# Sheaf edge loop: 80 of 125 columns summed on TensorE instead of 70, column sums laid between the equality sums, 16-bit source rows

## The reference

```python
h = jnp.maximum(_layernorm(x), 0.0)                     # (12500, 16)
xs, xd = h[src], h[dst]                                 # per edge, 16 values each
def reflection(a, b):
    return jax.nn.relu(jnp.concatenate([a, b], 1) @ W1.T + b1) @ W2.T + b2
def householder(v):
    vn = v / jnp.maximum(jnp.linalg.norm(v, axis=1, keepdims=True), 1e-12)
    return jnp.eye(16)[None] - 2.0 * vn[:, :, None] * vn[:, None, :]
F_s, F_d = householder(reflection(xs, xd)), householder(reflection(xd, xs))
L_sd = -jnp.einsum('eki,ekj->eij', F_s, F_d)
coef = deg_inv_sqrt[src] * deg_inv_sqrt[dst]
msg_s = coef[:, None] * jnp.einsum('eij,ej->ei', L_sd, xd)
msg_d = coef[:, None] * jnp.einsum('eji,ej->ei', L_sd, xs)
out = h - zeros.at[src].add(msg_s) - zeros.at[dst].add(msg_d)
x = x + jax.nn.relu(out)
```

## Time and profile before

| what | value |
|---|---|
| median of three runs | 23530.96 us |
| span of the profiled execution | 23516.1 us |
| TensorE busy | 18959.3 us (81%) |
| GpSimd (POOL) busy | 17392.8 us (74%) |
| VectorE (DVE) busy | 13526.5 us (58%) |
| ScalarE (ACT) busy | 2368.9 us (10%) |
| sheaf edge loop, first gather to last equality sum | 7792.6 to 14909.0 us |
| granted TensorE clock, mean of the span | 0.882 |

### The profile page before, as it was taken

The page is one execution under the profiler, slowest core; times in us unless marked ns, Lnnn a source line. Parts: engine busy times, 40 slices in busy tenths (PEclk is TensorE's granted clock), DMA queues, the critical chain, the costliest instruction groups (busy, mean ns, idle before and its releaser), DMA issues. The chain is left out here.

```text
span 23516.1 us, 304821 instructions
## 1 busy us (share of the span) xinstructions
PE 18959.3 (81%) x105910; PEld 12094.2 (51%) x105910; DVE 13526.5 (58%) x25320; ACT 2368.9 (10%) x5716; POOL 17392.8 (74%) x15021
## 2 busy tenths in 40 slices
PE   0688882789995388888888888679999998899997
PEld 0344441344442255555555555367777765555556
DVE  2788883455554266666556555445555552677772
ACT  0000000000000011111111111011111111111111
POOL 5777774777775788888888888478888880777775
PEclk9888885899997688888888888779999997999998
DMA  2222221112121111111222111123333321788884
GB/s 96 51 61 61 61 60 20 40 42 47 41 47 27 27 32 32 32 32 32 35 37 36 32 32 30 30 53 47 52 49 48 50 34 54 236 251 251 250 250 127
DMA packets 1968267, 1657.06 MB, mean 70 GB/s; under 512 B 780455, under 2 KB 1732934, under 8 KB 1949718
## 3 DMA queue, kind: packets, MB, share of 16 engines
q0 software_dynamic: 889216, 465.71, 14.3%
q10 hardware_dynamic: 821300, 579.22, 7.9%
q1 hardware_dynamic: 256354, 594.03, 7.5%
HBM read 953.63 MB, written 684.18 MB: 70 GB/s over the span
## 5 line engine op out<-in xcount | busy, mean ns | idle before, releaser
L1347 PE MATMUL node_sums<-placed_row,lane_values 128*128 128x392 bf16 x34500 | 6165.9, 338 | 534.3 <-DVE placed_row L1335 534.3
L1405 POOL DMA_INDIRECT acc<-column_sums,sum_rows x3375 | 5663.3, 1678 | 1193.1 <-issue 1140.1
L803 POOL DMA_INDIRECT gathered<-gat_table,src_index x4810 | 4835.3, 1005 | 1496.3 <-issue 1471.0
L1347 PEld LDWEIGHTS node_sums<-placed_row,lane_values 128*128 128x128 bf16 x34500 | 3455.8, 102 | 2962.7 <-DVE placed_row L1335 557.2
L1626 POOL DMA_INDIRECT gathered<-sheaf_table,src_index x3125 | 3402.1, 1089 | 960.2 <-issue 942.9
L2409 POOL DMA_INDIRECT gathered<-message_table,src_index x2381 | 2362.0, 992 | 727.5 <-issue 725.1
L1010 PE MATMUL lanes_ps<-S,table_parts 128*128 128x512 bf16 x9828 | 2272.4, 394 | 334.3 <-DVE S L875 334.3
L1335 DVE TENSOR_SCALAR placed_row<-iota_rows_f,src_row 128x1568 bf16<-128x1568 f16 x2875 | 1799.7, 651 | 1119.5 <-PE node_sums L1347 1090.3
L1010 PE MATMUL lanes_ps<-code_onehot,table_parts 128*128 128x512 bf16 x9828 | 2210.5, 386 | 154.7 <-DVE code_onehot L875 154.5
L1010 PEld LDWEIGHTS lanes_ps<-S,table_parts 128*128 128x128 bf16 x9828 | 985.3, 102 | 1558.3 <-DVE S L875 320.3
L1010 PEld LDWEIGHTS lanes_ps<-code_onehot,table_parts 128*128 128x128 bf16 x9828 | 972.5, 100 | 1332.3 <-DVE code_onehot L875 161.9
(11 more groups left out here) (484 smaller groups left out, 22192.5 us busy)
## 6 DMA issues: line engine op xcount, KB each, us to landing
message_rows<-gathered ACTq DMA_DIRECT2D x250, 1600.0 KB, 11.4
src_rows<-src_rows SPq DMA_DIRECT2D x200, 640.0 KB
src_rows<-src_rows SPq DMA_DIRECT2D x125, 960.0 KB
code_rows<-src_code_rows SPq DMA_DIRECT2D x360, 256.0 KB, 3.3
gat_rows<-scanned ACTq DMA_DIRECT2D x25, 3375.0 KB
gathered<-gat_table,src_index POOLq DMA_INDIRECT x4810
acc<-column_sums,sum_rows POOLq DMA_INDIRECT x3375, 3.1
gat_rows<-scanned ACTq DMA_DIRECT2D x25, 2125.0 KB, 6.8
```

The lines of the kernel that those rows point to most:

```text
L803: g.indirect_dma_start(G[b][:, j, :], None, tab, bass.IndirectOffsetOnAxis(ap=IX[b][:, j:j + 1], axis=0)).then_inc(s_g[b], 16)
L1347: last = pe.matmul(o.acc[:, m, 0:Q8 // 4], lane, o.OW[r][:, m * (Q8 // 4):(m + 1) * (Q8 // 4)], start=first(k, 1) and i == 0 and part == 0 ...
L1405: g.indirect_dma_start(self.acc[i], bass.IndirectOffsetOnAxis(ap=o.IXS[b][:, j:j + 1], axis=0), o.SV[b][:, j, :], None, compute_op=ALU.add ...
```

## The change

`MT` becomes 80, so GpSimd scatters 45 columns a chunk (nine rounds of 14 gathers and 5 scatters), and `late_tiles` are columns 40 to 59 as before, `sum_tiles` 60 to 69, `last_tiles` 70 to 79. The ten `sum_tiles` are laid between the 16 equality groups, on TensorE behind group g and on VectorE before the equality of group g + 2 (none stands at g = 0, 2, 5, 8, 10 and 13). In that stretch VectorE also does the products, the multiplication L1826 and the scans, which stood before it. The parts and the counts get buffers of their own, so lane values are made right before their first one-hot, with four lane buffers instead of five. The equalities of groups 0 and 1 are written before L1817. The source rows are int16 in DRAM and in SBUF.

```diff
-MT = 70
+MT = 80
+TAIL = 10
-        self.src_rows = self.dram("src_rows", (EP, P))
+        self.src_rows = self.dram("src_rows", (EP, P), I16)
-        o.ROW = [sb(f"src_rows{b}", [P, width * ACCS, P]) for b in range(2)]
+        o.ROW = [sb(f"src_rows{b}", [P, width * ACCS, P], I16) for b in range(2)]
...
-            late_tiles = range(SG * ACCS, MT - 2 * ACCS)
-            last_tiles = range(MT - 2 * ACCS, MT)
+            late_tiles = range(SG * ACCS, MT - 2 * TAIL)
+            sum_tiles = range(MT - 2 * TAIL, MT - TAIL)
+            last_tiles = range(MT - TAIL, MT)
+            beside = [sum_tiles[g * len(sum_tiles) // o.sums:(g + 1) * len(sum_tiles) // o.sums] for g in range(o.sums)]
+            SCANS = [range((g - 2) * D // 12, (g - 1) * D // 12) if 2 <= g < 14 else range(0) for g in range(o.sums)]
+            parts = sb("product_parts", [P, PARTS, MT, D], BF16)
...
                             last.then_inc(o.s_sum, 1)
+                            if not first(k, 1):
+                                for i in beside[g]:
+                                    self.tile_sum(pe, o, k - 1, 1 - b, i)
...
                         def ahead(q):
-                            for t in opens[q]:
-                                self.lane_values(v, o, k - 1, 1 - b, t, parts)
-                            for i in tiles[q] if q < SG else range(SG * ACCS, (SG + 1) * ACCS):
+                            place(range(q * ACCS, (q + 1) * ACCS))
+
+                        def place(columns):
+                            for i in columns:
+                                if i % ACCS == 0:
+                                    self.lane_values(v, o, k - 1, 1 - b, i // ACCS, parts)
                                 self.onehot_dve(v, o, k - 1, 1 - b, i)
...
-                        if not first(k, 1):
-                            self.lane_values(v, o, k - 1, 1 - b, MT // ACCS - 1, parts)
...
                         w(v.tensor_tensor(Q[:, :, 0:D], Q[:, :, 0:D], XX[:, :, D:2 * D], ALU.add))
-                        late(1)
+                        late(3)
+                        for g in range(o.nq):
+                            self.equal(v, o, k, b, g)
                         w(v.tensor_tensor(Q[:, :, D:2 * D], Q[:, :, D:2 * D], XX[:, :, 0:D], ALU.add))
-                        late(1)
                         v.tensor_copy(VAL[:, :, D:DW], bcast(self.order_w[:].unsqueeze(1), [P, EQC, 3]))
                         w(v.tensor_tensor(VAL[:, :, 0:D], Q[:, 0:EQC, 0:D], bcast(DP[:, 0:EQC].unsqueeze(2), [P, EQC, D]), ALU.mult))
                         v.sem_inc(s_val, 1)
...
+                        for g in range(o.sums):
+                            if g == 0:
+                                w(v.tensor_tensor(VP, Q[:, SC:CH, 0:D], bcast(DP[:, SC:CH].unsqueeze(2), [P, MT, D]), ALU.mult))
+                            if g == 1:
+                                w(v.tensor_tensor(Q[:, :, D:2 * D], Q[:, :, D:2 * D], bcast(NP_.unsqueeze(2), [P, CH, D]), ALU.mult))
+                                if not first(k, 2):
+                                    v.wait_ge(s_o[b], m - 16)
+                            for f in SCANS[g]:
+                                ins = v.tensor_tensor_scan(OUT[b][:, :, f], sm, Q[:, :, D + f], OUT[1 - b][:, CH - 1, f:f + 1], ALU.mult, ALU.add)
...
+                            if not first(k, 1):
+                                place(beside[g])
+                            if g + o.nq < o.sums:
+                                self.equal(v, o, k, b, g + o.nq)
+                        if not first(k, 1):
+                            place(last_tiles[:ACCS])
+                            self.lane_values(v, o, k - 1, 1 - b, last_tiles[ACCS] // ACCS, parts)
+                            v.wait_ge(o.s_svh, k * (MT // ACCS))
                         self.lanes(v, w, o)
```

More of the change, by code:

```diff
@@ L21 @@
 I32 = mybir.dt.int32
+I16 = mybir.dt.int16
 BF16 = mybir.dt.bfloat16
@@ L258, in setup @@
             s_g2, s_g3 = self.dsem("samples_in"), self.dsem("edges_in")
-            turned = [sb(f"src_turned{i}", [P, P], F32, c) for i in range(2)]
+            turned = [sb(f"src_turned{i}", [P, P], I16, c) for i in range(2)]
             turned16 = [sb(f"src_code_turned{i}", [P, 2, P], F16, c) for i in range(2)]
@@ L1276, in tile_buffers @@
         o.mt, o.OW, o.ring, o.lanes = mt, onehot, len(onehot), lanes
+        assert 2 * (mt // ACCS) % lanes == 0
         o.LOI = sb("src_bits", [P, mt], I32)
@@ L1560, in sheaf_edges @@
             o = self.scatter_buffers(c, SC, 2, 2)
+            assert o.sums == 16 and TAIL == 2 * ACCS and (MT - TAIL) % ACCS == 0 and MT - 2 * TAIL > (SG + 1) * ACCS
             flat = Q[:].rearrange("p c f -> p (c f)")
-            self.tile_buffers(c, o, MT, [sb(f"placed_row{i}", [P, Q8], BF16)[:] for i in range(ACCS)], (MT - SG * ACCS) // ACCS - 1,
+            self.tile_buffers(c, o, MT, [sb(f"placed_row{i}", [P, Q8], BF16)[:] for i in range(ACCS)], 4,
                               V[:].rearrange("p c f -> p (c f)")[:, 0:Q8])
@@ L1768, in late @@
                             if not first(k, 1):
-                                for i in range(at[0], min(at[0] + n, MT - 2 * ACCS)):
-                                    self.onehot_dve(v, o, k - 1, 1 - b, i)
+                                place(range(at[0], min(at[0] + n, late_tiles[-1] + 1)))
                                 at[0] += n
@@ L1805, in compute @@
                         w(v.tensor_tensor(Q[:, :, 0:D], V[:, 0:CH, 0:D], XX[:, :, D:2 * D], ALU.mult))
-                        late(1)
+                        late(2)
                         w(v.tensor_tensor(Q[:, :, D:2 * D], V[:, 0:CH, D:2 * D], XX[:, :, 0:D], ALU.mult))
-                        late(1)
+                        late(2)
                         w(v.tensor_reduce(tt[:], pair(Q[:]), AX.X, ALU.add))
@@ L1821, in compute @@
                         v.sem_inc(s_val, 1)
-                        late(2)
-                        w(v.tensor_tensor(VP, Q[:, SC:CH, 0:D], bcast(DP[:, SC:CH].unsqueeze(2), [P, MT, D]), ALU.mult))
-                        late(1)
-                        self.lanes(v, w, o)
-                        w(v.tensor_tensor(Q[:, :, D:2 * D], Q[:, :, D:2 * D], bcast(NP_.unsqueeze(2), [P, CH, D]), ALU.mult))
-                        late(2)
-                        if not first(k, 2):
-                            v.wait_ge(s_o[b], m - 16)
@@ L1830, in compute @@
-                        for f in range(D):
-                            ins = v.tensor_tensor_scan(OUT[b][:, :, f], sm, Q[:, :, D + f], OUT[1 - b][:, CH - 1, f:f + 1], ALU.mult, ALU.add)
-                        w(ins)
-                        assert at[0] >= MT - 2 * ACCS or first(k, 1)
-                        v.sem_inc(s_done, 1)
-                        for g in range(o.sums):
-                            self.equal(v, o, k, b, g)
-                        if not first(k, 1):
-                            for i in last_tiles[:ACCS]:
-                                self.onehot_dve(v, o, k - 1, 1 - b, i)
+                        assert at[0] > late_tiles[-1] or first(k, 1)
```

18 lines of the change are left out of this document (7 added, 11 removed).

## The result

| | before | after |
|---|---|---|
| median of four runs each | 23529.51 us | 23644.11 us |
| lowest to highest | 23491.98 to 23560.06 | 23622.22 to 23651.88 |
| span of the profiled execution | 23516.1 us | 23620.5 us |
| mean granted clock | 0.882 | 0.896 |

The changed kernel is slower by 115 us: ratio 1.0048, 95% interval 1.0035 to 1.0060. The forecast was +174 us, so the sign and the order of magnitude are right, and the forecast is half as large again as what came.

The account below looks back on a forecast made before the run. GpSimd bounded at 284.3 us a chunk; after, the VectorE-TensorE loop would, at 195.5 + 63 + 31.5 = 290.0. With +125, +18, +11 and +19.9, together +174 us: 23705 us, range 23360 to 23900.

Parts of the forecast that it names:

- First piece: Chunk start to the first equality sums: 195.5 us, where it was 213.0, since work moved out of it.
- Second piece: Equality sums with ten columns between: 63 us, the middle between 49.2 at 2.4 GHz and 76.5 at 1.2 GHz.
- The opening: Start of the equality sums: VectorE needs 7.5 us before column 60 can start, leaving TensorE some 5 us empty.
- the end without a low clock: Equality sums with ten columns, all at 2.4 GHz: 7.5 + 36.7 + 5 = 49.2 us.
- the mixture: Groups and columns interleaved in the equality stretch: clock expected to alternate, so the middle, 63 us, was taken.
- Third piece: Last group to next chunk's start: 19.7 us of VectorE work and handover, then 11.8 for five columns; 31.5 us.
- 16-bit rows: int16 source rows, in loads, equality, setup and layer 2: costed at zero, within 15 us; equality 0.83 us.
- rival 4: Equalities on 16-bit rows take half the time: up to 4 us a chunk, loop 286, 23610 us; chance 0.07.
- 1, the high clock throughout: Clock stays at 2.4 GHz in the equality stretch: loop 276.2 us, -155, 23375 us; chance 0.20.
- 2, the low clock throughout: Clock stays at 1.2 GHz in the equality stretch: loop 303.5 us, +499, 24030 us; chance 0.11.
- 3, GpSimd as the bound: GpSimd still bounds the sheaf edge loop: 264.5 us a chunk, -425, 23106 us; chance 0.05.
- VectorE's order between 11111 and 11165: VectorE's sequence ahead of the equality sums, cited against TensorE running with hardly any gap, which a GpSimd bound needs.

Follow-up runs that it names:

- e3: Changed kernel plus idle matmuls of a constant in TensorE's gaps after six groups and fifty before the last five columns: 23401.57 us, ratio 0.9933 to before.
- e5: Changed kernel plus only the 30 idle matmuls after group 1, in the opening gap: 23625.62 us, ratio 1.0018 to before.
- e1: Kernel before with only the source rows in int16 (DRAM table and row buffers): 23543.36 against 23562.76 us, ratio 0.9992.
- e8: e6 with the tail's VectorE work moved among the groups and each one-hot made a group ahead: 23211.16 us, ratio 0.9861 to before.
- e2: Changed kernel with columns 60 to 69 behind the equality groups instead of between them: 23554.22 us, ratio 0.9994 to before.
- e6: Changed kernel with VectorE's order altered: column 60 first, multiplication at group 3, scans from group 4, products at group 14: 23622.5 us, ratio 1.0019 to before.
- e4: Changed kernel with 70 columns on TensorE instead of 80, new order kept: 23511.11 us, ratio 0.9979 to before.

## Why the forecast was right in sign and half as large again

**GpSimd.** Right: its instructions cost 125 x 1.415 + 45 x 1.948 = 264.5 us a chunk, the forecast's 264.5, and it idles 23.7 us (over 20 forecast). What it idles for was named wrongly. The wait is put down to VectorE's L1862, the end of the index chain that its scatters need, and not to its own index load: in the chunk shown that load is issued at 11259.43, the chain's last step starts at 11275.90, and GpSimd goes on at 11277.01. Nothing in the sum hung on that.

**First piece.** Right: 195.4 us against 195.5. In the chunk shown, 1.1 us longer than the mean, the last columns of the blocks begin 141.6 us after its start (142.2 forecast) and the rest takes 55.0 us (53.3 forecast). That the piece is 17.0 us shorter than before and that the wait for the gathers was 17.0 us is a coincidence: that wait, gone as forecast, stood in the third piece.

**Second piece.** The mechanism is right, the size was off by 4.4 us: 58.6 against 63. Its parts held. The opening took 11213.97 - 11206.54 = 7.4 us for 7.5; the end without a low clock is 48.4 by e3 for 49.2; the four waits before columns in the chunk shown (0.71, 3.00, 0.71 and 0.34 us) make 4.8 for 5. The term that was mis-sized is the mixture: I took the middle between the two ends, and the trace has (58.6 - 48.4) / (76.5 - 49.2) = 0.37 of the way to the low one. With a clock of 0.76 over the groups TensorE is at the high level for (0.76 - 0.50) / 0.50 = half of the time, and the faster half does more than half of the work: a middle in time is not the middle between the two durations. Nor were the waits even: five of 1 us were forecast, and one of them is 3 us. A reading beside the sum was wrong too: behind 11131.10 the kernel before runs 17 slow matmuls, not some 14, before the clock comes back; no term hung on it.

That a stretch of short rests makes the clock go back and forth, which the Trainium skill says in "TensorE: Matmul & The Clock Gate", "A second HAM failure mode: psum-queue depth-cycling", is what this trace shows: windows at 0.50, 0.95 and 0.50 again inside 58 us, and 27 of 69 falls behind waits of at most 0.71 us. e5 shows it with the opening gap filled.

**Third piece.** 33.7 us against 31.5, and here a wait was overlooked. The changed kernel's VectorE waits 16.4 us in ten chunks, five times some 3.2 us, before L1749, with nothing that releases it (the row in the list of waits above). It comes in each second chunk, as the loop over two chunks turns round. The kernel before has it too, by its list of waits over the same stretch:

```profile
DVE dots L1743 <- issue: 17.2, 5, 3.5
```

There the wait for the gathers, which follows it, hid it; once that wait is gone the pause is on the path. In the changed kernel the third piece takes 35.8 us in the chunks with the pause and 31.7 in the others; the chunk of the earlier trace rows that I read is one without it. Of the 4.1 us between them, 2.9 come ahead of column 75 in the chunk looked at (a wait of 12.48 us there instead of 9.57), and TensorE has a pause of its own at the same turn:

```profile
9856.46 0.65 PE L1648 MATMUL xyT_sums_ps<-ident,src_dst 128*128 128x128 f32 x4 [0.93 <-issue]
```

The turn of the loop so makes some 2.0 of the 2.2 us by which the forecast of this piece was too short. "Where a stall goes, what is late next" should have been asked of this row as well. What fills the pauses, no run tells.

**16-bit rows.** Right: e1. The equality takes 0.822 us with one 16-bit operand (0.825 in e1) where 0.826 was the 32-bit form's, so rival 4 is out. In layer 2 nothing changed: TensorE busy 1913.9 us of 2000 after and 1909.0 before, between 16000 and 18000.

**The sum.** By TensorE's transposes at the chunks' starts, before and after:

| | forecast | measured |
|---|---|---|
| chunks 2 to 24 | 22 x 5.7 = +125 | 6328.4 - 6254.9 = +73.5 |
| chunk 1 | +18 | 294.4 - 271.6 = +22.8 |
| chunk 24 to the end of its groups | +11 | 253.1 - 247.1 = +6.0 |
| from there to the last column | +20 | 185.7 - 163.6 = +22.0 |
| in all | +174 | +124.3 |

The 51 us too much in the first line are 22 x (0.1 + 4.4 - 2.2), by the three pieces. The other 20 us down to the 104.4 between the two spans lie outside these rows: the first chunk began 10.1 us earlier and took 1.5 us less, and from the last column to the end it was 8.4 us less. Between the profiled executions of this study the first chunk's start moves by far more than that, from 7945 (after, e8) to over 8050 us, though the layer ahead of it does the same work in all of them.

**The rivals.** 1, the high clock throughout: did not come by itself, but e3 makes it, and the loop is the forecast 276.2 (276.3). 2, the low clock throughout: no. 3, GpSimd as the bound: not with this order; e8 has it. The argument against it, "VectorE's order between 11111 and 11165", was a poor one. e8 leaves that order as it is and finds the time in the other two pieces. Its first piece is 198.9 us on average, even 3.4 us longer than the changed kernel's: with the wait for the gathers back, the first one-hots of a chunk come late, and TensorE waits for them behind its first transposes, as in the kernel before.

**The cause, then.** Shown: with ten columns more, GpSimd stops being the bound (waits of after), the low clock costs 10 us of the second piece (e3), and laying columns between groups in this order costs 4.6 us a chunk over laying them behind (e2). Shown too: the long gaps come from VectorE's long instructions standing between an equality and the next one-hot (e6 moved the gap with the instruction, e8 took it away). They are not the whole of it, since the clock also falls behind waits of 0.71 us (e5). e8 changed the places of the one-hots, the lane values and the products at once, so which of these moves gave how much is not shown. The number of columns is not at fault: e8 has 80 as well. Not tried: 80 columns with 32-bit source rows. By the sizes in the code the parts' own buffer takes 3 x 80 x 16 x 2 = 7680 bytes of each partition, and the halved rows give back 2 x 10 x 128 x 2 = 5120 in this loop; so the 16-bit rows, worth nothing in time, may be what lets the parts have a place of their own.

## What to carry to other kernels

When two engines hand work back and forth in short steps, make each operand one step ahead and put the long instructions behind it, not before it; here the same work in another order was worth 18 us of 288. When a bound is moved off one engine, look in the trace for the small waits that its stall hid, in more than one turn of the loop: here a pause in each second chunk, which made that chunk's third piece 4.1 us longer. And price a stretch that may run at either clock from both ends, then look at all its waits and not only at the longest: filling the longest gap gave back 2.0 of the 10.2 us that the low clock cost, because here the clock also fell behind waits of 0.71 us.

## What was not expected of the hardware

- Extra matmuls made the kernel faster: 110 more a chunk to keep TensorE busy, and the chunk fell from 287.7 to 276.3 us (e3).
- Equality sums alone never brought the high clock back in any of the 25 chunks of before, e1 or e2, though TensorE shows as 100% busy all through: in e2 thirteen groups in a row ran at 2.15 us each. The window over them:

```profile
11234.00:11261.00 27.00, 27.00 (x129) 0.50 0.42 93
```

  The same groups take 1.0 to 1.2 us apiece between columns at the high clock (2.30 us for two in e8, as a row).
- The clock fell behind waits of TensorE of 0.71 us and less: twice in most chunks of e5, before any longer wait of its stretch.
- The gathers' mean duration is not fixed: 1.066, 1.097, 1.110 and 1.132 us in e4, before, after and e8, for the same 125 columns. At 125 a chunk the ends differ by 8 us, which is more than the 3.4 us by which the two kernels' chunks differ. The other runs lie between. What makes them longer or shorter was not tried.
